# First attention by heads of 64, with the weights as they are, in a gated cross-attention kernel on Trainium2

## What is computed

```python
x = x + tanh(g_xattn[0]) * attention_1(ctx, layernorm(x), mask)   # 16 heads of 64, inner width 1024
x = x + tanh(g_ffn[0])   * ffn_1(layernorm(x))                    # 128 -> 512, butterflies, gelu, -> 128
x = x + tanh(g_xattn[1]) * attention_2(layernorm(x), ctx)         # 16 heads of 8, the best 32 of 77 keys
x = x + tanh(g_ffn[1])   * experts(layernorm(x))                  # router, one of 8 experts a token

# attention_1(x=ctx, latents=layernorm(x), mask)
xn, lat = layer_norm(x, g1, b1), layer_norm(latents, g2, b2)
q  = lat @ Wq                                   # 128 x 1024
kv = concatenate([xn, lat]) @ Wkv               # 205 x 2048, split into k and v
w  = softmax(where(mask, (q * s) @ (k * s).T, -max))     # a head: 128 x 205, s = 64 ** -0.25
out = (w @ v, heads side by side) @ Wout        # 128 x 128
```

## Time and profile before

| | |
|---|---|
| median of 3 runs | 796.79 us (795.46 to 798.51) |
| the profiled execution | 796.77 us, of which the span from first to last instruction 795.0 us |
| busy, share of the span | PE 90%, PEld 72%, DVE 72%, ACT 58%, POOL 57% |
| mean granted TensorE clock | 0.927 of full speed |

### The profile page before, as it was taken

How to read it: one execution, slowest core, us unless ns; L and a number is a source line. 1 busy time by engine, 2 the same in 40 slices (tenths; PEclk the granted TensorE clock), 3 DMA queues, 4 the chain that set the end, 5 groups by cost and what they waited for, 6 DMA issues and landing times.

```text
span 795.0 us, 17992 instructions
## 1 busy us (share of the span) xinstructions
PE 717.2 (90%) x4442; PEld 575.6 (72%) x4442; DVE 574.9 (72%) x3758; ACT 463.9 (58%) x1226; POOL 452.4 (57%) x705
## 2 busy tenths in 40 slices
PE   5899989999999999999999999999999965752896
PEld 5766677778787877777787787777877854541886
DVE  2755525788887979797888887879788899964222
ACT  2265567686767676767677676768576734220221
POOL 6275747665665747474847565656566445642243
PEclk9689999999999999999999999999999985555799
DMA  6200099930000000000000000000000000101772
GB/s 196 63 1 1 1 292 304 298 113 1 2 2 0 0 0 0 0 0 0 0 0 0 0 0 0 0 0 0 0 1 2 2 0 15 47 15 53 209 219 67
DMA packets 38531, 37.85 MB, mean 48 GB/s; under 512 B 3632, under 2 KB 34247, under 8 KB 38482
## 3 DMA queue, kind: packets, MB, share of 16 engines
q1 hardware_dynamic: 32984, 27.76, 12.7%
q10 hardware_dynamic: 3994, 6.36, 2.8%
q0 software_dynamic: 1504, 3.17, 1.1%
HBM read 16.28 MB, written 21.45 MB: 47 GB/s over the span
## 4 chain that ended last, share of the span: by engine, by line
PE 44%; DVE 30%; ACT 11%; issue 7%; SPq 3%; POOL 2%; DMA 2%; another core or an unknown queue 1%; DVEq 1%; ACTq 0%; POOLq 0%
DVE raw L1537 12%; DVE m L1531 9%; PE bank L854 8%; PE bank L726 6%; PE bank L881 4%; PE bank L842 4%; ACT prob L1188 4%; DVE negmax L1479 3%; PE bank L1160 3%; PE bank L871 3%; PE bank L1170 3%; PE bank L872 2%; ACT raw L1188 2%; PE bank L903 2%; PE bank L940 2%
## 5 line engine op out<-in xcount | busy, mean ns | idle before, releaser
L1537 DVE MATCH_REPLACE8 raw<-m,raw 128x77 f32<-128x77 f32 x1024 | 220.1, 222 | 0.0
L1531 DVE MAX8 m<-raw 128x8 f32<-128x77 f32 x1024 | 189.3, 226 | 1.1 <-DVE raw L1537 0.6
L1188 ACT ACTIVATE prob<-bank,negmax 128x205 f32<-128x205 f32 x256 | 108.3, 428 | 99.0 <-DVE negmax L1479 98.7
L498 POOL TENSOR_TENSOR prob<-prob,inv 128x820 f32<-128x820 f32 x64 | 99.4, 1553 | 64.4 <-DVE inv L1484 64.4
L1479 DVE TENSOR_REDUCE negmax<-bank 128x2 f32<-128x410 f32 x128 | 74.2, 580 | 80.9 <-PE bank L854 79.0
L517 POOL TENSOR_TENSOR raw<-raw,m 128x616 f32<-128x616 f32 x64 | 77.8, 1216 | 93.3 <-DVEq L1513 93.3
L854 PE MATMUL bank<-kvT,g_sb 128*128 128x205 f32 x512 | 123.8, 365 | 0.0
L854 PEld LDWEIGHTS bank<-kvT,g_sb 128*128 128x128 f32 x512 | 83.0, 190 | 10.2
L940 PEld LDWEIGHTS bank<-v,p1T 77*128 77x128 f32 x512 | 73.4, 213 | 14.7 <-issue 4.5
L1537 DVE MATCH_VALUE_LOAD raw<-m,raw 128x8 f32 x1024 | 78.0, 76 | 0.0
L940 PE MATMUL bank<-v,p1T 77*128 (+1 forms) x512 | 70.6, 265 | 8.2 <-ACT p1T L1188 3.9
(11 more groups left out here) (232 smaller groups left out, 1337.7 us busy)
## 6 DMA issues: line engine op xcount, KB each, us to landing
z_sorted<-no_row SPq DMA_DIRECT2D x1, 17415.0 KB, 64.8
b_w<-in_L_ffn_W ACTq DMA_DIRECT2D x23, 256.0 KB
z_tile<-z_sorted SPq DMA_DIRECT2D x23, 129.0 KB, 2.6
w<-in_L_ffn_W SPq DMA_DIRECT2D x8, 256.0 KB, 4.6
raw<-in_L_xattn_Wkv SPq DMA_DIRECT2D x2, 512.0 KB, 5.7
xs<-in_x SPq DMA_DIRECT2D x1, 960.0 KB, 6.9
cx<-in_ctx SPq DMA_DIRECT2D x1, 577.5 KB
raw<-in_L_xattn_Wq SPq DMA_DIRECT2D x1, 512.0 KB, 3.7
```

The source lines that it names most:

```text
L498: g.tensor_tensor(p, p, inv[:, 4 * q:4 * q + 4].unsqueeze(2).to_broadcast([128, 4, KV]), ALU.mult).then_inc(s["p_norm"], 1)
L1188: return nc.scalar.activation(dst, src, f, **kw)
L1531: v.max(m8[:, h, r, :], sw[:, h, src, :]).then_inc(s[name], 1)
L1537: v.match_replace(sw[:, h, 1, :], m8[:, h, r, :], sw[:, h, src, :], TAKEN)\
```

## The change

The weights are no longer merged. `Wq`, `Wk`, `Wv` and `Wout` stay in SBUF as loaded and are operands in every round: `queries_in` (8 heads a call), `keys_in` (4 heads a call) and `values_in` (8 heads, context or latents) write to bank GZ or OA, and ACT copies the results out. `w_psum` and `w_ready` count these ten steps of a batch. A head has 64 rows or columns, so two heads share the 128 partitions: `scores` works on a quad with a head in the lower and one in the upper half of the rows, `attend` with a head in either half of the output, and `project_out` is one chain of eight products at the end. The 14 jobs that merged go.

A quad's scores fill both banks S0 and S1 at once (`SC`), in the even slots; the next quad's `scores` waits until all exponentials of the last are done. `maxima` are taken two at a time in the even slots, `exps` of both pairs run in the slot behind on ACT. The mask is kept as rows 0 and 64 of an otherwise zero tile; `stage_mask` copies one batch's on POOL.

Further moves: the loads stand in another order on SP; the statistics of batches 4 to 15 are taken in round 1 and not ahead of the loop; E's residual, statistics and root go from slot 3 to slot 4 and its `normal` into `between`; `close_top` stands elsewhere; `inverses(A, 1)` goes into `between`; `copy_keys` is gone; several tiles lie elsewhere in SBUF.

```diff
-        J_A = 6
-        J_BIAS = J_A + QUADS
+        J_BIAS = 0
         J_BFT = J_BIAS + 1
         J_WEXP = J_BFT + 1
-        J_B = J_WEXP + 1
-        J_BF = J_B + QUADS
+        J_BF = J_WEXP + 1
...
             sp.dma_start(cx[:, 0, :], t["ctx_1024"][0]).then_inc(s["ld_first"], 16)
+            sp.dma_start(w_exp[:, :], t["L0_ffn_W_exp"]).then_inc(s["ld_wexp"], 16)
+            for n, name in enumerate(("Wq", "Wk", "Wv", "Wo")):
+                sp.dma_start(l1_in[:, n, :], t[f"L1_xattn_{name}"]).then_inc(s["ld_l1w"], 16)
+            sp.dma_start(cx[:, 1:NB, :], t["ctx_1024"][1:NB].rearrange("b n d -> n b d")).then_inc(s["ld_c"], 16)
...
             sp.dma_start(wq_in, t["L0_xattn_Wq"]).then_inc(s["ld_wq"], 16)
...
+            def queries_in(b, name, j, n):
+                dst = (GZ, OA)[name == "OA"]
+                free(name)
                 reach(pe, "kvt_ready", b, 1)
...
+                for c in range(4):
+                    last = mm(dst[:, 128 * c:128 * c + 128], wq_in[:, 512 * j + 128 * c:512 * j + 128 * c + 128],
+                              kvT[:, NK:KV], start=True, stop=True)
...
+            def keys_in(b, name, j, n):
...
+                for c in range(2):
+                    at = 256 * j + 128 * c
+                    last = mm(dst[:, KV * c:KV * c + KV], wkv_in[:, at:at + 128], kvT[:, :], start=True, stop=True)
...
+            def values_in(b, name, rows, j, n):
...
+                r0, nr = (0, NK) if rows == "ctx" else (NK, S)
+                mm(dst[0:nr, :], kvT[:, r0:r0 + nr], wkv_in[:, INNER + 512 * j:INNER + 512 * j + 512], start=True, stop=True)\
+                    .then_inc(s["w_psum"], 1)
...
+            def scores(b, q, n):
+                reach(pe, "exp_done", b, 2 * q)
+                reach(pe, "w_ready", b, n)
...
+                rows = [slice(0, 64), slice(64, 128)]
+                for u in range(2):
+                    dst = SC[:, u, 0:2 * KV].rearrange("p (h n) -> p h n", h=2)
+                    mm(dst[:, :, 0:NK], ones_rows[rows[u], :],
+                       mask_now[rows[u], :].unsqueeze(1).to_broadcast([64, 2, NK]), start=True, stop=False,
+                       skip_group_check=True)
+                for r in range(2):
+                    for u in range(2):
+                        last = mm(SC[:, u, KV * r:KV * r + KV], q_sb[rows[u], q // 2, 2 * (q % 2) + r, :],
+                                  k_sb[rows[u], q % 2, r, :], start=False, stop=(r == 1), skip_group_check=True)
+                        if r == 1:
+                            last.then_inc(s["s_psum"], 1)
...
+            def attend(b, name, q, lag, n):
...
+                for c in range(2):
+                    for v, p, last_part in ((v_ctx, ptc, False), (v_lat, ptl, True)):
+                        for u in range(2):
+                            h = 4 * q + 2 * c + u
+                            last = mm(dst[64 * u:64 * u + 64, 128 * c:128 * c + 128], v[:, DH * h:DH * h + DH],
+                                      p[:, 2 * c + u, :], start=not last_part, stop=last_part, skip_group_check=True)
...
+            def project_out(b):
...
+                for c in range(NC):
+                    last = mm(OA[:, 0:D], att_T[:, c, :], wout_in[:, 128 * c:128 * c + 128], start=(c == 0),
+                              stop=(c == NC - 1))
```

ACT's queue in a round, as far as it changes (slots 5 to 7 and 0; the others alike):

```diff
                     if slot == 0:
                         if A is not None:
                             keys_out(A)
                         if A2 is not None:
-                            attended(A2, 2)
-                        if A is not None:
-                            projected(A, 0)
+                            attended(A2, GZ, 2)
+                        if A is not None:
+                            queries_kept(A, OA, 0, 0)
+                            keys_kept(A, GZ, 0, 1)
                         if E is not None:
                             second_probs_out(E, 3)
-                        if A is not None:
-                            exps(A, 0)
...
                     if slot == 5:
                         if A is not None:
+                            values_kept(A, GZ, v_ctx, 1, 7)
+                            exps(A, 4)
                             probs_out(A, 1)
-                            projected(A, 3)
...
                         if A is not None:
+                            keys_kept(A, OA, 3, 8)
                             exps(A, 5)
...
                     if slot == 6:
                         if A is not None:
-                            attended(A, 1)
+                            attended(A, GZ, 1)
...
-                        if A is not None:
+                    if slot == 7:
+                        if A is not None:
+                            probs_out(A, 2)
                             exps(A, 6)
-                    if slot == 7:
-                        if A is not None:
-                            probs_out(A, 2)
-                        if A is not None:
+                            values_kept(A, OA, v_lat, 1, 9)
                             exps(A, 7)
```

POOL and DVE:

```diff
                         if A2 is not None:
                             rsqrt(A2, f_mv, f_rs, "f_stats", "f_eps", "frs_ready")
+                        if A is not None:
+                            normalise(A, 1)
+                    if slot == 4:
                         if E is not None:
                             rsqrt(E, c_mv, c_rs, "c_stats", "c_eps", "crs_ready")
-                        if A is not None:
-                            normalise(A, 1)
-                    if slot == 4:
                         if A2 is not None:
...
-                    if slot in (3, 7) or (slot in (1, 5) and A is None):
-                        close_top()
...
+                    if i == 1 and 1 <= slot <= 6:
+                        input_stats(2 * slot + 2, 2 * slot + 4, (0, 1))
...
-                    if A is not None:
+                    if A is not None and slot % 2 == 0:
                         maxima(A, slot)
-                    if slot in (1, 5):
-                        close_top()
+                        maxima(A, slot + 1)
...
-                    if slot == 3 and E is not None:
+                    if slot == 4 and E is not None:
                         reach(dve, "o1_psum", E, 1)
                         reach(dve, "xo_added", E, 1)
                         residual(E, last_x(E), M[:, 0:D], 1, "x3_ready")
                         statistics(E, last_x(E), c_st, c_mv, "x3_ready", "c_stats")
...
+                    if slot in (1, 3, 7):
+                        close_top()
```

More of the change, by code:

```diff
@@ L282, in flamingo_kernel, with move_jobs @@
         PLACE_AT[20, 6] = tuple(range(*ROUTES[1]))
-        def job_heads(q):
-            return [8 * (q // 2) + q % 2 + 2 * n for n in range(4)]
-        def job_part(w, q):
-            h0 = job_heads(q)[0]
-            return w[:, h0:h0 + 7:2, :]
         def wait_job(eng, k):
             eng.wait_ge(s["set_act" if k % 2 == 0 else "set_dve"], k // 2 + 1)
-        def move_jobs(eng, jobs, copy, scaled, biased, added=None):
+        def move_jobs(eng, jobs, copy, biased, added=None):
             done = s["set_dve" if jobs[0] % 2 else "set_act"]
@@ L676, in step @@
                     if slot == 4:
+                        if E is not None:
+                            rsqrt(E, c_mv, c_rs, "c_stats", "c_eps", "crs_ready")
                         if A2 is not None:
@@ L702, in step @@
                             normalise(A, 3)
+                        if P is not None:
+                            if i == 0:
+                                pool.wait_ge(s["c_mask"], 3)
+                            stage_mask(P)
                     for b in PLACE_AT.get((i, slot), ()):
@@ L835, in keys_T @@
                 read_next("M", "kvt_ready", 1, 1)
-            def project(b, q):
-                free("GZ")
+            def queries_in(b, name, j, n):
+                dst = (GZ, OA)[name == "OA"]
+                free(name)
                 reach(pe, "kvt_ready", b, 1)
-                for n in range(4):
-                    last = mm(GZ[:, 128 * n:128 * n + 128], a_w[:, 4 * q + n, :], kvT[:, NK:KV], start=True, stop=True)
-                last.then_inc(s["g_psum"], 1)
-                read_next("GZ", "g_ready", 1, q + 1)
@@ L1037, in step @@
                         if A is not None:
-                            project(A, 0)
-                        if A2 is not None:
-                            project_out(A2, 2)
+                            queries_in(A, "OA", 0, 0)
+                            keys_in(A, "GZ", 0, 1)
                         if E is not None:
@@ L1048, in step @@
                         if A is not None:
-                            project(A, 1)
-                            scores(A, 1)
+                            keys_in(A, "OA", 1, 2)
                         if E is not None:
                             contexts(E, 3)
+                        if A is not None:
```

(13 more changed lines are left out.)

291 lines of the change are left out of this document (131 added, 160 removed).

## The result

The changed kernel takes 848.52 us (843.96 to 850.77, four runs), 1.0642 times the kernel before [1.0593 to 1.0691, 95%]. The forecast was 803 (784 to 820): slower, as said, but by 52 us and not by 6. The profiled execution has a span of 847.3 us against 795.0.

The account below looks back on a forecast made before the run. A closed chain of four stretches over DVE, ACT and PE, 37.87 us a round, was taken as the bound, not PE alone. 796.77 - 10.3 (start) + 16.5 (eleven rounds, 1.5 us each) = 803 us, range 784 to 820.

Parts of the forecast that it names:

- PE's sum: PE's work per round: -2.9 us if half-array products overlap, the case taken, +3.2 us if none do.
- Stretch 1: DVE from a round's first maximum to slot 4's maximum: 16.5 us, before 18.23.
- Stretch 2: Slot 4's maximum to second_exps(C, 3): 8.64 us, before 5.78, because POOL's queue makes below_max(C, 3) late.
- Stretch 3: ACT's queue from second_exps(C, 3) to the kvT copy: 9.05 us, before 8.98.
- Stretch 4: From kvT over down, keys and scores to the first maximum: about 5.2 us, before 4.88.
- PE's 2.9 us are hidden: it now waits: In full rounds PE's 2.9 us saving shortens nothing; PE waits for keep_top(C, 2)'s p1 and for kvT.
- The start: Up to the full rounds: -10.3 us, 3.3 from POOL's earlier roots, the rest from the first three rounds.
- they get 2, 2.5 and 2.5: First three rounds, where PE was taken as the limit: gains in us out of PE's 2.9.
- POOL isn't late: Rival: below_max(C, 3) stays off the chain, slot 4 to second_exps(C, 3) takes 7.1 us; 786.5 us, chance 0.28.
- PE the limit: Rival: PE sets the round and its 2.9 us come through in every round; 755 us, chance 0.07.
- No overlap: Rival: half-array products in scores and attend don't overlap; 827 us, chance 0.08.
- The pair of score banks: Rival: the next scores wait for all four exponentials, costing 1 us more a round; 814 us, chance 0.10.

Follow-up runs that it names:

- with POOL relieved: Kernel after with stage_inputs moved behind below_max(C, 3) and normalise(A, 2) on POOL from the second batch on: 1.0672 times the kernel before.
- with the exponentials back: Kernel after with exps(A, 0), (A, 2), (A, 4), (A, 6) back in ACT's slots 0, 2, 4, 6: 817.03 us.
- `kvT` first: Kernel after with second_scores_out(3) and second_exps(0) moved behind ACT's kvT copy: 832.44 us with late exponentials, 797.14 us with the even ones back in their earlier slots.
- the exponentials back and the waits filled: Kernel after with even exponentials back in slots 0, 2, 4, 6 and nine unread products a round in PE's waits around kvT: 804.43 us.
- the run with halves apart: The 804.43 us kernel (even exponentials back, nine unread products) with scores and attend products issued all of one half first, then the other: 828.11 us.
- The best kernel run: Kernel after, even exponentials back, kvT copied first, POOL's first mask copy, coefficients and up_part(0) early, roots of batches 1 to 3 behind both down_parts: 788.35 us.
- only `exps(A, 6)` back: Kernel after with only exps(A, 6) back in ACT's slot 6, behind the GELU; the other three even exponentials stay one slot later: 821.87 us.

## Why the prediction was right and wrong

- **PE's sum.** Right: alternating halves overlap, also for `attend`, where no row of before showed it. In clean rounds without filler PE is busy 34.10 of 37.84 us where it was 37.25: 3.15 less, forecast 2.9.
- **Stretch 1.** Right, 16.29 for 16.5: `f_z` takes 0.35 as priced, and waits 0.49 us for POOL's root instead of 0.85.
- **Stretch 2.** Right in size, the reason half right. POOL ends `below_max` right behind `stage_inputs`, as drawn, but ACT arrives in the same tenth of a microsecond, and with POOL relieved the stretch is still 8.60. So the sign named for it, an exponential within 0.1 us of the end of `below_max`, came (0.12) and couldn't tell the two engines apart. That POOL decides shows only with the exponentials back, by 0.18 us.
- **Stretch 3.** The failed step is "the 0.21 of idle time goes (the maxima come a slot early)". It took the exponentials' move as a pure gain and never placed `exps(A, 6)` and its table load against the wait for `ptc`. 9.93 for 9.05; in clean rounds all that hangs on the move is 39.98 - 38.72 = 1.26 us.
- **Stretch 4 and "PE's 2.9 us are hidden: it now waits".** The failed step with the greatest share, 21.7 of the 28.9 us. It put the price of a wait of PE at nothing. One of the two waits foreseen came (for `kvT`, 0.79 us), the one for `p1` did not in a full round, and two unforeseen ones stand ahead of it (0.62 and 1.60 us); the clock falls behind them and PE's next 3.4 to 6.8 us run at half speed, just on the way from `kvT` to the first maximum. 7.30 for 5.2, on average 7.17; with the clock up it is 5.15, filled or not. That this is the forecast's value is in part luck: the terms written there (0.40 + 1.16 + 0.90 - 0.16 + 0.80 + 0.57 + 1.35) add up to 5.02.
- **The start.** That `kvT` comes 9 us earlier is right (26.95 for 36.44), but "3.3 is gained" from POOL's earlier roots was not: the roots do start 4.1 us earlier (28.98 for 33.09) and the first stage of `wd` 4.5 (34.63 for 39.17), but the mask's copy went to the end of the same queue, and the first maximum comes only 1.4 us earlier (41.18 for 42.56), the second `kvT` 1.1. Then "they get 2, 2.5 and 2.5" fell too: with the clock nearly clean (`kvT` first) rounds 2 to 4 are 35.6, 34.9 and 36.2 us, before 36.2, 34.3 and 35.6, so PE wasn't their limit; what was, no run shows. With the exponentials back and the waits filled the fifth `kvT` comes at 177.67, so these two causes carry 7.2 of the 18.3 us missed at the start, and the other 11 are what these two gains were overrated by (2.0 up to the second `kvT`, 9.0 behind it).
- **Rivals.** "POOL isn't late" (786.5) didn't come: its stretch of 7.1 let ACT follow 1.9 us behind DVE, and with POOL relieved ACT still takes 8.60. PE the limit (755) is out: in a round of 37.84 PE has 3.7 us idle. No overlap (827) is out; the run with halves apart has its cost by chance near that sum. The pair of score banks stays open: `scores(A, 2)` waits 1.4 to 1.55 us for the exponentials in the kernel after, rounds got 4 us shorter with it still there, and what it costs wasn't tried. That 804.4 is next to the forecast's 803 is partly luck: its rounds take 7.3 us less than forecast over eleven, its start 11 more.

The best kernel run keeps the new projections and takes 788.35 us, 10 us less than the kernel before on the same chip (798.63). Whether the start's moves would do as much for the old projections wasn't run.

## What to carry to other kernels

Work taken from a busy TensorE isn't free time: where it turns into waits, count what a fall of the clock costs behind each, and first of all look whether ScalarE's order (a table load behind a wait, copies ahead of the one that all wait for) can close them. When an instruction is moved past another that changes the activation table, move the table load in the sum as well. And behind a wait of 8 us look for the next engine's wait of nearly the same end before forecasting its removal.

## What the runs showed of the hardware

- **The clock falls behind short waits.** Behind the first of the eleven rounds none here is over 2 us (ahead of it `attend` waits 2.54 in the kernel after). By PE's waits around `kvT` (us) and the rounds of eleven with a stretch at 1.2 GHz: 0.62 + 1.60 + 0.79, eleven, seven of them twice as long; 0.62 + 1.59, nine; one wait of 1.91 in the old kernel, seven; 0.62 + 0.75 + 0.78, six; 0.63 + 0.46 + 0.78 (only `exps(A, 6)` back), five; 0.63 + 0.75, one; 0.18 + 0.48, none; 0.31 in the kernel before (row below), none. A clean and a half-clock round with the same waits stand side by side, so these waits make the fall likely and don't settle it; what decides in a single round no run shows. A wait that stands alone was harmless at 1.41 to 1.55 us: `scores(A, 2)` of the kernel after has one in each of the eleven rounds, and the clock stays at 1.00 behind all of them.

```profile
328.78 1.16 PE L903 MATMUL bank<-wd,f_h 128*128 128x128 f32 x8 [0.31 <-ACT kvT L1188]
```

  The Trainium skill (TensorE: Matmul & The Clock Gate, A second HAM failure mode: psum-queue depth-cycling) tells of a kernel whose clock swings because of short idle times between groups of products. The trace agrees, and gives a price: 1.6 us a stretch of 3.4.
- **Products that nobody reads can pay.** Nine a round, 2.0 us more of PE's work (36.17 for 34.17 us busy in clean rounds of 38.7, exponentials back), took 22 us off the changed kernel and 13 off the one with the exponentials back.
- **Half-array products overlap across a few instructions**, not only with their neighbour: eight score instructions take 0.96 us with the halves in two runs of four (0.90 in turn), the sixteen of `attend` in two runs of eight 1.6 (1.1).
